# A mixture-of-experts tail: the output product as three fp32r products, with weights divided per block and register loads moved

## The reference, cut to what matters

```
x = x + attention(layernorm(x))                     # x: (8, 256, 256)
n = layernorm(x)
w, idx = top_k(n @ gate, 2); w = softmax(w)
h0, h1 = n @ w0[e], n @ w1[e]                       # 256 -> 512, for each expert e
out = sum over the 2 chosen e of  w_e * ((silu(h0) * h1) @ wo[e])      # 512 -> 256
x = x + out
```

## Time and profile before

| what | value |
|---|---|
| median of 3 runs | 823.74 us (823.67 to 824.26) |
| the profiled execution | 824.96 us, of it the span of the instructions 823.0 us |
| PE busy | 759.4 us, 92% of the span |
| DVE, ACT, POOL busy | 509.8, 479.9, 420.8 us |
| mean granted PE clock | 0.976 of full speed |

### The profile page before, as it was taken

One profiled execution on the slowest core, in us unless ns is written; L12 is line 12 of the kernel. 1 busy time (PEld: TensorE's weight loads), 2 busy tenths in 40 slices (PEclk: granted clock), 3 DMA queues, 4 the chain that ended last, 5 costly groups with the idle time before them and its releaser, 6 DMA issues.

```text
span 823.0 us, 19373 instructions
## 1 busy us (share of the span) xinstructions
PE 759.4 (92%) x5952; PEld 646.7 (79%) x5952; DVE 509.8 (62%) x2098; ACT 479.9 (58%) x1537; POOL 420.8 (51%) x674
## 2 busy tenths in 40 slices
PE   3689999999999999999999999986598999999994
PEld 2578887988888888889888888875477778888883
DVE  5788677767666757757766767776545754333331
ACT  2477876776777777677677777656244442222220
POOL 0456664656565555556465665542314454555442
PEclk9899999999999999999999999988999999999998
DMA  6432122212202302131221221218832222222330
GB/s 195 141 113 94 51 74 61 65 40 66 75 31 61 78 32 65 42 72 42 64 69 41 65 72 33 53 43 295 292 115 44 45 49 46 47 41 45 53 51 6
DMA packets 52851, 61.05 MB, mean 74 GB/s; under 512 B 10544, under 2 KB 45616, under 8 KB 52752
## 3 DMA queue, kind: packets, MB, share of 16 engines
q1 hardware_dynamic: 45264, 50.46, 21.1%
q0 software_dynamic: 7488, 9.36, 6.7%
HBM read 26.21 MB, written 9.32 MB: 43 GB/s over the span
## 4 chain that ended last, share of the span: by engine, by line
PE 76%; DVE 11%; ACT 5%; issue 4%; DMA 2%; SPq 1%; POOL 0%; POOLq 0%; DVEq 0%; ACTq 0%
PE h L1505 13%; PE projected L379 10%; PE attn_out L524 10%; PE probsT L484 9%; PE scores L471 8%; PE yb L1524 8%; PE heads_out L503 5%; PE projected L400 3%; PE heads_out L506 2%; PE tg L1515 2%; PE projected L357 2%; ACT exps L596 2%; ACT exps L594 1%; DMA raw<-w_attn 1%; PE tx L1497 1%
## 5 line engine op out<-in xcount | busy, mean ns | idle before, releaser
L898 POOL TENSOR_SCALAR probs<-exps,inv_sums 128x128 f32<-128x128 f32 x256 | 97.9, 382 | 227.8 <-DVE inv_sums L729 180.9
L603 ACT COPY pT<-probsT 128x384 f32<-128x384 f32 x256 | 121.7, 476 | 85.2 <-PE probsT L484 85.1
L484 PE MATMUL probsT<-identity,probs 128*128 128x128 f32 x768 | 132.1, 282 | 13.3 <-ACT pT L603 12.4
L594 ACT ACTIVATE exps<-masked,neg_max 128x128 f32<-128x128 f32 x256 | 102.8, 402 | 61.2 <-DVE neg_max L723 61.1
L596 ACT ACTIVATE exps<-masked,neg_max 128x256 f32<-128x256 f32 x256 | 127.2, 497 | 0.0
L899 POOL TENSOR_SCALAR probs<-exps,inv_sums 128x256 f32<-128x256 f32 x256 | 123.0, 480 | 0.0
L1715 POOL DMA_INDIRECT out<-y,to_token x39 | 61.9, 1586 | 110.8 <-DVE y L1645 90.8
L379 PE MATMUL projected<-xT_hi,w 128*128 128x256 f32 x512 | 112.7, 301 | 5.9 <-DVE k_sin L711 3.6
L1505 PE MATMUL h<-experts_w,xsT_hi 128*128 x312 | 108.9, 431 | 4.7 <-issue 3.3
L484 PEld LDWEIGHTS probsT<-identity,probs 128*128 128x128 f32 x768 | 88.9, 143 | 27.5 <-POOL probs L899 15.5
L723 DVE CUSTOM_DVE_ANT_0 masked<-scores,tables 128x256 f32<-128x256 f32 x256 | 107.5, 420 | 0.2 <-issue 0.2
(11 more groups left out here) (179 smaller groups left out, 1627.5 us busy)
## 6 DMA issues: line engine op xcount, KB each, us to landing
qT<-rotated SPq DMA_DIRECT2D x256, 64.0 KB, 2.1
kT<-k_cos SPq DMA_DIRECT2D x64, 128.0 KB, 3.3
experts_w<-w_in SPq DMA_DIRECT2D x16, 512.0 KB, 5.8
raw<-w_attn SPq DMA_DIRECT2D x20, 256.0 KB, 3.2
experts_w_out<-w_out SPq DMA_DIRECT2D x8, 512.0 KB, 7.1
out<-x_all SPq DMA_DIRECT2D x8, 256.0 KB, 2.3
xn_rows<-raw SPq DMA_DIRECT2D x8, 256.0 KB, 3.3
x_all<-x SPq DMA_DIRECT2D x1, 1792.0 KB, 11.4
```

The source lines that it names most:

```text
L484: mm = nc.tensor.transpose(p_bank[:, at:at + P], probs[:, h, at:at + P], ident[:, :])
L594: nc.scalar.activation(exps[:, h, 0:P], masked[:, h, 0:P], ACT.Exp, bias=neg_max[:, h, 0:1], scale=-1.0, accum_out=sums[:, h, 0:1])
L603: nc.scalar.copy(pT[:, n % 2, h, :], p_bank[:, 0:3 * P]).then_inc(pT_done, 1)
L898: nc.gpsimd.tensor_scalar(probs[:, h, 0:P], exps[:, h, 0:P], inv_sums[:, h, 0:1], 1.0, ALU.mult, ALU.mult)
```

## The change

Four things change.

1. From block 15 (`THREE_FROM`) on, output(j) is done by `output_parts`: 12 fp32r matmuls over 256 columns in the order gT_hi x second_hi, gT_hi x second_lo, gT_lo x second_hi.
2. For that, each block's 128x1024 output weights are divided when the block comes: ACT casts them to `second_hi`, DVE subtracts to get `second_lo`. There is one buffer of each. ACT's cast waits until output(j-1) is done, and both load the owner into a register first. `g_copy` casts to `gT_hi`, and DVE computes `gT_lo` = `tg` - `gT_hi`.
3. For all blocks, PE loads the owner of j+1 once, between the second and third matmul of h0(j), and computes the 8 addresses of its first weights after the first four matmuls of h1(j). Block 16, whose successor's owner comes later, loads it at the end of its pass.
4. Some SBUF tensors (`lane_hot`, `block_codes`, `gT`) move into the region that attention frees, and the new tensors lie in their place; a semaphore `owners_late` tells that the late owners are written.

```diff
+THREE_FROM = 15
         def output(j, expert):
+            if j >= THREE_FROM:
+                output_parts(j)
+                return
...
+        def output_parts(j):
+            i = j - THREE_FROM
+            pe.wait_ge(gT_done, j + 1)
+            pe.wait_ge(second_lo_done, i + 1)
+            pe.wait_ge(y_done, j)
+            n = 0
+            for g, part in ((gT_hi, second_hi), (gT_hi, second_lo), (gT_lo, second_hi)):
+                if n == 2 * MT:
+                    pe.wait_ge(gT_lo_done, i + 1)
+                for k in range(MT):
+                    mm = nc.tensor.matmul(yb[:, 0:EMB], g[:, k * P:(k + 1) * P], part[:, k * EMB:(k + 1) * EMB],
+                                          start=(n == 0), stop=(n == 3 * MT - 1))
+                    n += 1
...
         for j in range(1, BLOCKS):
-            last, expert = owner(j - 1), owner(j)
+            last, expert = expert, following
+            def next_owner(n):
+                nonlocal following
+                if n == 1 and j < LAST and j != EARLY_BLOCKS - 1:
+                    following = owner(j + 1)
+            def next_addresses(n):
+                if n < 4 and j < LAST and j != EARLY_BLOCKS - 1:
+                    first_addresses(following, n)
             pe.wait_ge(xT_lo_done, j + 1)
             pe.wait_ge(gated_done, j)
             slots_ready(j)
-            hidden(j, expert, 0)
+            hidden(j, expert, 0, next_owner)
             g_transposes(j - 1)
-            hidden(j, expert, 1)
+            hidden(j, expert, 1, next_addresses)
...
     def scalar(act):                       # in g_copy, and at the end of pass j
+            if j >= THREE_FROM:
+                act.wait_ge(yb_ps, j)
+                nc.scalar.copy(gT_hi[:, :], tg[:, :]).then_inc(gT_done, 1)
+                return
+        def second_split_hi(j):
...
+            act.wait_ge(yb_ps, j)
+            expert = act.value_load(r["owners"][0:1, j:j + 1], min_val=0, max_val=EXPERTS - 1)
+            nc.scalar.copy(second_hi[:, :], w_out[:, bass.ds(expert * WO, WO)]).then_inc(second_hi_done, 1)
     def vector(dve):
+        def g_lo(j):
+            dve.wait_ge(gT_done, j + 1)
+            nc.vector.tensor_tensor(gT_lo[:, :], tg[:, :], gT_hi[:, :].bitcast(F32), ALU.subtract).then_inc(gT_lo_done, 1)
+        def second_split_lo(j):
+            dve.wait_ge(second_hi_done, j - THREE_FROM + 1)
+            expert = dve.value_load(r["owners"][0:1, j:j + 1], min_val=0, max_val=EXPERTS - 1)
+            nc.vector.tensor_tensor(second_lo[:, :], w_out[:, bass.ds(expert * WO, WO)], second_hi[:, :].bitcast(F32),
+                                    ALU.subtract).then_inc(second_lo_done, 1)
         for j in range(BLOCKS):
+            if j >= THREE_FROM:
+                second_split_lo(j)
+                g_lo(j)
             if j < LAST:
                 gate_rows(j + 1)
```

More of the change, by code:

```diff
@@ L922, in attention, with route @@
     return {"sync": sync, "tensor": tensor, "scalar": scalar, "vector": vector, "gpsimd": gpsimd}
-def route(nc, ctx, t, r):
+def route(nc, ctx, ctx_shared, t, r):
     def sb(name, shape, dt=F32):
@@ L930, in sem, with shared @@
         return ctx.enter_context(nc.semaphore(name))
+    def shared(name, shape, dt):
+        return ctx_shared.enter_context(nc.sbuf_tensor(name, shape, dt))
     TE = TILES * EXPERTS
@@ L983, in route @@
     row_lane = sb("row_lane", [P, 2, TILES])
-    lane_hot = sb("lane_hot", [P, 2, TILES, P], BF16)
-    block_codes = sb("block_codes", [P, 2, TILES, 2, LATE_BLOCKS], BF16)
     pair_of = sb("pair_of", [P, 3, BLOCKS])
+    lane_hot = shared("lane_hot", [P, 2, TILES, P], BF16)
+    block_codes = shared("block_codes", [P, 2, TILES, 2, LATE_BLOCKS], BF16)
+    r["gT"] = shared("gT", [P, MLP], F32)
     tables_in = sem("route_tables_in")
@@ L1007, in route @@
     xn_last_out = sem("xn_last_out")
+    owners_late = sem("owners_late")
     weights_done = sem("weights_done")
@@ L1342, in owners_of @@
         wait_own(dve, nc.vector.tensor_reduce(owner[:, 0:n], later[:, 0:n, :], AX.X, ALU.add))
-        nc.vector.tensor_scalar(r["owners"][:, first:first + n], owner[:, 0:n], -1.0, None, ALU.add)
+        ins = nc.vector.tensor_scalar(r["owners"][:, first:first + n], owner[:, 0:n], -1.0, None, ALU.add)
+        if part == 1:
+            ins.then_inc(owners_late, 1)
     def early_owners(dve):
@@ L1435, in route @@
                 late_rows=late_rows, late_lanes=late_lanes, block_hots=block_hots, group_codes=group_codes,
-                owners_of=owners_of, read_pairs=read_pairs, slot_lo=slot_lo, gathers_ready=gathers_ready)
+                owners_of=owners_of, read_pairs=read_pairs, slot_lo=slot_lo, gathers_ready=gathers_ready,
+                owners_late=owners_late)
 def experts(nc, ctx, sems, t, r, rt):
@@ L1445, in sem @@
         return sems.enter_context(nc.semaphore(name))
+    second_hi = sb("second_hi", [P, WO], F32R)
+    second_lo = sb("second_lo", [P, WO], F32R)
+    gT_hi = sb("gT_hi", [P, MLP], F32R)
+    gT_lo = sb("gT_lo", [P, MLP], F32R)
+    sb("unused", [P, 192])
     ew = r["ew"] = sb("experts_w", [P, EXPERTS, 2, WI], F32R)
@@ L1474, in experts @@
     gT_done = sem("gT_done")
+    gT_lo_done = sem("gT_lo_done")
+    second_hi_done = sem("second_hi_done")
+    second_lo_done = sem("second_lo_done")
     yb_ps = sem("yb_ps")
@@ L1498, in x_transposes, with first_weights, first_addresses, hidden @@
             mm.then_inc(xT_ps, 1)
-        def hidden(j, expert, which):
+        def first_weights(expert, part, c):
+            return w[:, bass.ds(expert * 2 * WI + part * WI + c * MLP, MLP)]
+        def first_addresses(expert, n):
+            for c in (2 * n, 2 * n + 1):
+                pe.lower_ap(first_weights(expert, c % 2, c // 2))
+        def hidden(j, expert, which, between):
             ps, done = ((h0, h0_ps), (h1, h1_ps))[which]
@@ L1505, in hidden @@
                     mm = nc.tensor.matmul(ps[:, :], x[:, j % RING, k * P:(k + 1) * P],
-                                          w[:, bass.ds(expert * 2 * WI + part * WI + (which * KT + k) * MLP, MLP)],
+                                          first_weights(expert, part, which * KT + k),
                                           start=(n == 0), stop=(n == 3 * KT - 1))
+                    between(n)
                     n += 1
@@ L1513, in g_transposes @@
             pe.wait_ge(gated_done, j + 1)
+            if j > THREE_FROM:
+                pe.wait_ge(gT_lo_done, j - THREE_FROM)
             for k in range(MT):
@@ L1525, in output @@
                                       start=(k == 0), stop=(k == MT - 1))
+            mm.then_inc(yb_ps, 1)
+        def output_parts(j):
[11 more added lines that the diff above has]
+                    n += 1
             mm.then_inc(yb_ps, 1)
@@ L1544, in tensor, with nothing @@
         slots_ready(0)
-        hidden(0, expert, 0)
-        hidden(0, expert, 1)
+        def nothing(n):
+            return None
+        hidden(0, expert, 0, nothing)
+        hidden(0, expert, 1, nothing)
         x_transposes(1)
+        following = owner(1)
         for j in range(1, BLOCKS):
-            last, expert = owner(j - 1), owner(j)
+            last, expert = expert, following
[6 more added lines that the diff above has]
+                    first_addresses(following, n)
             pe.wait_ge(xT_lo_done, j + 1)
@@ L1561, in tensor @@
             output(j - 1, last)
+            if j == EARLY_BLOCKS - 1:
+                pe.wait_ge(rt["owners_late"], 1)
+                following = owner(j + 1)
             if j == 1:
@@ L1570, in tensor @@
         g_transposes(LAST)
-        output(LAST, owner(LAST))
+        output(LAST, expert)
     def scalar(act):
@@ L1586, in g_copy @@
             act.wait_ge(gT_ps, j + 1)
+            if j >= THREE_FROM:
+                act.wait_ge(yb_ps, j)
+                nc.scalar.copy(gT_hi[:, :], tg[:, :]).then_inc(gT_done, 1)
+                return
             nc.scalar.copy(gT, tg[:, :]).then_inc(gT_done, 1)
+        def second_split_hi(j):
+            if j == THREE_FROM:
+                act.wait_ge(r["pairs_done"], 2)
+                act.wait_ge(rt["owners_late"], 1)
+                for place in range(EXPERTS):
+                    act.wait_ge(r["w_out_in"][place], 16)
+            act.wait_ge(yb_ps, j)
+            expert = act.value_load(r["owners"][0:1, j:j + 1], min_val=0, max_val=EXPERTS - 1)
+            nc.scalar.copy(second_hi[:, :], w_out[:, bass.ds(expert * WO, WO)]).then_inc(second_hi_done, 1)
         def side_work(j):
@@ L1612, in scalar @@
                 x_copy(j + 1)
+            if j >= THREE_FROM:
+                second_split_hi(j)
             side_work(j)
@@ L1766, in program @@
             "order": sb("order", [P, EXPERTS], I32),
-            "gT": sb("gT", [P, MLP]),
             "both_weights": sb("both_weights", [P, 2]),
@@ L1776, in program @@
         }
-        rt = route(nc, outer, t, r)
-        sems = outer.enter_context(ExitStack())
```

(2 more changed lines are left out.)

## The result

The changed kernel takes 833.73 us (median of 4, 830.61 to 834.56), beside 824.0 for the kernel before in the same session (823.67 to 824.94); the ratio is 1.0115 [1.0096, 1.0135]. The profiled execution took 830.61, span 828.8, mean granted clock 0.976.

A forecast was written before the change was run, and what follows sets the result against it. PE was taken as the bound, with a chain through DVE hardly shorter; after the change, a two-pass division loop. Terms 13.3 + 0.3 + 2.0 + 0.7 = 16.3 on 824.96 gave 841.3, less 1.2 for the median: 840.0 us, range 829 to 848.

The forecast's parts named there:

- Rival A: ACT and DVE: loads and division run beside other work, passes at the x_lo chain's 5.11; 821.9 us, chance 0.06.
- The loop through the division: Passes 16 to 37: D + R spans two passes, so 5.79 a pass against 5.18, 13.3 us slower.
- D: From output(j-1)'s end through ACT's and DVE's loads, division, gT_lo, gate_rows and x_lo to pass j+2's start: 6.03 us.
- R: PE's time from the start of pass j+2 to the end of its output(j+1): 5.54 us, 0.28 of it register load.
- The loads' price: Owner register load on ACT and DVE, from release to use: 0.83 us each, with 0.16 hand-over included.
- The x_lo chain: h1, multiplication by h1, x_lo, next h0: 5.11 us, so a faster PE alone gains at most 0.07 a pass.
- The gap in h0: PE stands for 0.28 us after h0's second matmul, waiting for the register load, when x_lo comes last.
- Rival B: PE has matmuls queued when its register load comes, so no gap: passes of 5.65, 836 us, chance 0.20.
- PE's saving: Output's matmuls: twelve fp32r ones take 1.44 us against 1.71 for eight float32, saving PE 0.27 a block.
- The end: After the passes: output(37) waits 0.3 for second_lo, and the last division and output cost 2.0 us more.
- Early passes: Passes 1 to 15: late-sequencer passes gain, six smooth ones lose about 0.2 each; sum +0.7 us, bounds -1.5 and +4.
- PE's busy share as a sign: Sign that the forecast is right: PE's busy share in the steady stretch falls to about 0.85.

The follow-up runs named there:

- loads_early_later: Changed kernel with ACT's and DVE's owner loads ahead of their waits and PE's register load moved from h0 into h1: 820.14 us, ratio 0.9957 to the kernel before.
- after: The changed kernel itself, with all four changes to the kernel before: 833.73 us, ratio 1.0115.
- loads_early: Changed kernel with only the owner's register loads on ACT and DVE put ahead of their waits: 822.47 us, ratio 0.9977 to the kernel before.
- load_later: Changed kernel with only PE's register load moved from h0 into h1, behind queued matmuls: 831.43 us, ratio 1.0079 to the kernel before.
- all_three_ahead: Changed kernel with loads ahead of waits, PE's load in h1, rows' work reordered from block 15, gathers one block earlier: 816.36 us, ratio 0.9910 to the kernel before.
- act_two_loads: Changed kernel with a second register load of the same owner on ACT before the cast: 847.61 us, ratio 1.0291 to the kernel before.
- before: The kernel before the change, unmodified: 824.0 us in the changed kernel's session.

## Why the prediction was right, and where its size was off

*Direction right, cause right in kind.* The time got longer by a chain that runs through ACT's and DVE's division, with each register load behind its wait. Rival A, loads beside other work, was false for the kernel as written; the runs with the loads ahead of their waits show that it needs just those moved lines (822.47 for A's 821.9), and that more comes out once PE's load is moved too (820.14). But the chain that binds is another than the one the prediction summed.

*The loop through the division: mis-sized, and not the one that binds.* The term 22 x 0.604 = 13.3 measured 7.48. The prediction wrote down D + R over two passes. In the profile after, D is 742.62 to 747.98, 5.36. R without the 0.19 in front of the output is 746.19 - 742.51 = 3.68, and with the output's 1.71 it is 5.39. Half the sum is 5.38, below the 5.47 of the one-buffer loop, which the prediction did not list. D came out 0.67 below its 6.03: the loads give 0.24 of it, the hand-over to h0 0.10, and the way from the subtraction's end to x_lo's 0.35, since it took 1.60 (746.32 to 747.92) instead of 0.69 + 1.26; the subtraction itself took 0.02 more. The second_lo starts 2.47 after the output's end, for 2.7 worked out. At the prediction's prices the one-buffer loop would have been 0.83 + 1.05 + 0.83 + 1.215 + 0.16 + 1.60 = 5.69. Against this the pass measured 0.22 less: the loads took 0.66 and 0.76 instead of 0.83 twice (-0.24), the hand-over to PE 0.06 instead of 0.16 (-0.10), and the output's matmuls 1.71 instead of 1.60 (+0.11).

That the forecast lay only 6 us above the measured time is thus in part luck: a loop that does not bind, with terms too dear, came near one that was not listed. No run made a second pair of buffers, which would cut the loop itself.

*The loads' price.* The 0.83 from release to use measured 0.66 on ACT and 0.76 on DVE. The 6.5 us that the prediction puts beside it for a load of 0.6 counts only those two engines; PE's load in R at the same price would add 3.3. The 0.05 for issuing two matmuls stands on no row.

*The x_lo chain: mis-sized.* The prediction held that a faster PE alone gains at most 0.07 a pass, as this chain takes 5.11. In loads_early_later it binds at 4.90: 3.10 instead of 3.20 up to h1's last matmul, and 0.06 instead of 0.16 from x_lo to h0. The 3.20 came from a pass in which PE itself was the bound, and the 0.16 from block 1.

*Beyond the steady passes.* 22 x (5.47 - 5.18) is 6.4; most of the other 1.1 lies in the three long passes of after. Pass 16 is the loop's first turn, and the first register load of each engine is longer: 470 ns on ACT and 549 on DVE, so that the cast begins 0.96 after the output's end, the subtraction 1.04 after the cast's, and PE's weight loads stand 1.29 in front of the output. With the two loads ahead of their waits (loads_early) pass 16 takes 5.12.

*The gap in h0: there, and without effect.* The third weight load comes 0.67 after the first instead of 0.44, so 0.23 against 0.28 (0.33 beside the 0.34 of load_later). But it is hidden in front of an output that waits for second_lo anyway (load_later). The prediction's R had it on the path. With the one-buffer loop gone it does show: most passes take 5.06 to 5.14 in loads_early and 4.88 to 4.92 in loads_early_later.

*Rival B* (836 without the gap) came out closer in time than the forecast, for the wrong reason: taking the gap away does not shorten the pass.

*PE's saving: right.* 0.27 less a block gives 5.18 - 0.27 = 4.91; where PE is the bound (all_three_ahead) the passes take 4.87.

*gT_lo, gate_rows and x_lo: right.* They stand back to back on DVE (746.23, 746.83, 747.50), and no wait for h1 is left between them.

*The end: right*, 2.3 for 0.3 + 2.0. The y_scales are 5.47 apart instead of the 5.7 worked out, which is 2.28 more than the 3.19 before.

*Early passes: +0.49 for +0.7*, but by luck and not by the terms named: smooth passes lost nothing (5.08, 5.17, 5.19 for passes 13 to 15, and 5.06, 5.39, 5.07 before), and kernels with the same early passes take from 95.05 (act_two_loads) to 95.62 (after) for passes 0 to 15.

*PE's busy share as a sign: wrong.* It is 0.99, not 0.85. The gap in h0 hides in the rows: the first two matmuls' modelled end (742.51 + 0.74 = 743.25) lies behind the start of the third (743.19). And PE's weight loads idle for only 0.19 before the output. A busy share with modelled ends could not tell this bound from PE's own; the length of a pass and the link output, cast, subtraction, output could.

## What to carry to other kernels

Where one buffer is filled, used and filled again, write down the loop through that buffer by itself (last use to fill to next use to its end) beside the longer loops: it binds from the first repetition and no averaging over passes softens it. Put a register load ahead of the wait whose data it doesn't need; behind it, each one is in the loop at full length. And a faster engine pays only when what feeds it is moved along: here the same three products gave +1.2%, then -0.4%, and, with the gathers a block earlier, -0.8% or -0.9%.

## What the runs showed of the hardware that was not expected

A register load does not cost one price: from release to the next instruction 0.66 us on ACT and 0.76 on DVE, of which 0.13 and 0.14 stay when the load stands ahead of the wait (loads_early_later). The load itself takes 278 and 304 ns, the arithmetic behind it 152 and 190. The Trainium skill ("Advanced Engine Details and Errata", "Clock Domains") lets the same count of cycles last a quarter longer on DVE's sequencer: 190 / 152 = 1.25 agrees for the arithmetic; the load is only 304 / 278 = 1.09 times as long.

POOL's scatters and gathers get longer beside DVE's subtraction. In before all 19 scatters of 700 to 800 us take 1.59 and gathers 0.98 or 0.99; in loads_early_later the scatter that starts at 742.08, 1.01 before the subtraction ends, takes 2.48, which is 0.89 more; in after the gather at 746.00, 0.32 before its end, takes 1.17, 0.18 more. DVE keeps its 1.22 to 1.23. The added time is what is left of the subtraction less 0.12 or 0.13 in all 18 gathers of after and all 19 scatters of loads_early between 700 and 800 us (with 0.25 to 1.05 left). A scatter that is already under way when the subtraction starts is not delayed: the one at 744.11 in after runs to 745.70 beside the subtraction from 745.09 and takes its 1.59. The Trainium skill ("SBUF — State Buffer", "Who interferes with whom") lets a DVE instruction with two SBUF inputs contend with a GpSimd one that reads SBUF; the numbers agree with an instruction of POOL that starts beside the subtraction standing until that is nearly done. That POOL's instruction reads SBUF there, and that this is the port and not another resource, was not separated.
